# The last norm's output on ScalarE, and the message bias as a row of the state

## The reference

```python
x = _layernorm(x + adj @ (x @ W0) + b0)            # first layer
x = _layernorm(x + fused_gcn(x[:, :25], adj))      # second, on 25 "nodes"
x = _layernorm(x + attention(x, adj))              # third: u = adj*exp(e+f+a_b), h' = u @ h / sum(u)
# fourth:
h = relu(bn(conv1(x))); x_conv = relu(bn(conv17(h)) + x)
s = x @ w_se.T + b_se                              # 3 features a node
A = exp(-|s_n - s_m|^2) * adj_mask
msg = relu(x @ w_msg.T + b_msg)                    # the message
x_nmp = A @ msg
z, r, n = gru(concat(x_conv, x_nmp), x)
x = _layernorm(x + (1 - z) * n + z * x)            # the last norm, the output
```

## Time and profile before

| | |
|---|---|
| median of 3 runs | 595.26 us (595.21 to 595.3) |
| profiled execution | 594.41 us |
| its span in the trace | 592.6 us |
| TensorE clock granted | 0.996 of full speed |
| busy share | PE 97%, DVE 83%, ACT 52%, POOL 19% |

### The profile page before, as it was taken

The page is one execution under the profiler, slowest core; times in us unless marked ns, Lnnn a source line. Parts: engine busy times, 40 slices in busy tenths (PEclk is TensorE's granted clock), DMA queues, the critical chain, the costliest instruction groups (busy, mean ns, idle before and its releaser), DMA issues.

```text
span 592.6 us, 11756 instructions
## 1 busy us (share of the span) xinstructions
PE 572.8 (97%) x3611; PEld 491.2 (83%) x3611; DVE 492.8 (83%) x1842; ACT 310.4 (52%) x641; POOL 112.8 (19%) x124
## 2 busy tenths in 40 slices
PE   6998999999999999999999999999999999999894
PEld 6896987978889797979788897979797988889584
DVE  3778968898989888888989898888889898989675
ACT  2316636546464555555554646465556556464342
POOL 3311130212112030212031211203020312112010
PEclk9999999999999999999999999999999999999998
DMA  7880041020020303030301103030303021000000
GB/s 187 288 284 2 2 145 49 2 79 32 19 89 0 107 0 107 0 107 0 104 3 42 65 0 107 0 107 0 107 0 105 2 66 42 19 2 0 19 19 18
DMA packets 33309, 34.47 MB, mean 58 GB/s; under 512 B 1668, under 2 KB 22539, under 8 KB 33154
## 3 DMA queue, kind: packets, MB, share of 16 engines
q1 hardware_dynamic: 32994, 34.01, 18.3%
q10 hardware_dynamic: 288, 0.13, 0.1%
HBM read 29.75 MB, written 4.39 MB: 58 GB/s over the span
## 4 chain that ended last, share of the span: by engine, by line
PE 81%; DVE 4%; issue 1%; ACT 0%; POOLq 0%; POOL 0%; DVEq 0%
PE bank L254 13%; PE bank L256 13%; PE bank L255 13%; PE bank L1757 9%; PE pair L254 6%; PE pair L256 6%; PE pair L255 6%; PE bank L1588 4%; PE bank L1599 2%; PE pair L1688 2%; PE bank L1693 2%; PE pair L1749 2%; PE bank L1653 1%; PE bank L1699 1%; PE bank L1683 1%
## 5 line engine op out<-in xcount | busy, mean ns | idle before, releaser
L1134 POOL TENSOR_TENSOR rs<-ve,neg_half 128x4 f32<-128x4 f32 (+1 forms) x60 | 57.1, 952 | 294.0 <-DVE ve L1309 261.1
L254 PE MATMUL bank<-cd_hi,w_hi 128*128 128x256 f32 x272 | 77.4, 285 | 0.0
L255 PE MATMUL bank<-cd_lo,w_hi 128*128 128x256 f32 x272 | 76.6, 282 | 0.0
L256 PE MATMUL bank<-cd_hi,w_lo 128*128 128x256 f32 x272 | 76.3, 281 | 0.0
L1757 PE MATMUL bank<-P,msg 128*128 128x512 f32 x128 | 58.6, 600 | 1.0
L254 PE MATMUL pair<-aT_hi,x_hi 128*128 128x512 f32 x128 | 52.6, 411 | 0.6 <-DVE x_lo L772 0.3
L254 PEld LDWEIGHTS bank<-cd_hi,w_hi 128*128 128x128 f32 x272 | 51.3, 189 | 1.5
L255 PEld LDWEIGHTS bank<-cd_lo,w_hi 128*128 128x128 f32 x272 | 51.3, 189 | 1.3
L256 PEld LDWEIGHTS bank<-cd_hi,w_lo 128*128 128x128 f32 x272 | 51.4, 189 | 0.0
L256 PE MATMUL pair<-aT_hi,x_lo 128*128 128x512 f32 x128 | 50.3, 393 | 0.0
L255 PE MATMUL pair<-aT_lo,x_hi 128*128 128x512 f32 x128 | 50.1, 391 | 0.0
(11 more groups left out here) (361 smaller groups left out, 1521.3 us busy)
## 6 DMA issues: line engine op xcount, KB each, us to landing
adj_nat<-in_adj_dram SPq DMA_DIRECT2D x16, 1024.0 KB, 5.9
x_nat<-in_x_dram SPq DMA_DIRECT2D x16, 256.0 KB, 2.9
xt<-in_x_dram SPq DMA_DIRECT2D x3, 1280.0 KB, 11.8
out_dram<-y_out SPq DMA_DIRECT2D x15, 256.0 KB, 2.4
hw<-in_L_gnn_W_dram SPq DMA_DIRECT2D x2, 640.0 KB, 6.7
xt<-in_L_gnn_conv_w_dram SPq DMA_DIRECT2D x1, 1088.0 KB, 10.2
aT<-in_adj_dram SPq DMA_DIRECT2D x5, 96.0 KB
nat_ih<-in_L_gnn_w_ih_dram SPq DMA_DIRECT2D x1, 384.0 KB, 6.0
```

What stands on the lines that cost most here:

```text
L254: nc.tensor.matmul(o, lh, rh, start=start, stop=False)
L255: nc.tensor.matmul(o, lh, rl, start=False, stop=False)
L256: return nc.tensor.matmul(o, ll, rh, start=False, stop=stop)
L1134: g.tensor_tensor(rs[i][:, 0:n], ve[i][:, 0:n], neg_half[:, 0:n], ALU.pow).then_inc(po_rs[i], 1)
```

## The change

There are two parts. In the turns in which graph b-1 and graph b are both there (1 to 15), ACT writes the last norm's output as an Identity with a scale `rs` and a bias `shift` for each node; DVE computes `less`, the negative means, directly behind the variances, and POOL multiplies `less` by `rs` into `shift`. PE and SP wait for ACT's output where they waited for DVE's. And the biases of message and s move into the weights: feature 0 of the state is replaced by the constant 1 (`x3M`, made by ACT from `x3T` with a scale and a bias for each partition), row 0 of the weights is replaced by the bias, and row 0's weight is subtracted from the other 127 rows, since the features sum to zero. So the two bias matmuls go, and the waits ahead of them move behind `out0`. In the first block two small loads come in among the early ones (`b_msg` as one more row of `vrows`, `b_se` as a column), eight small loads at the end of SP's list go, and so do one ACT and two DVE instructions that made `msg_bias`; three DVE instructions come in that prepare the weights, and on POOL two memsets go, one comes in, and two small instructions make `keep`.

```diff
+                sp.dma_start(vrows[BMSG:NROWS, :], a["L3_gnn_b_msg"].unsqueeze(0)).then_inc(q_row, 16)
+                sp.dma_start(vrows[HB:BMSG, :], a["L1_gnn_b1"]...).then_inc(q_row, 16)
...
+                sp.dma_start(nat_ws[0:3, 0:1], a["L3_gnn_b_se"].unsqueeze(1)).then_inc(q_ww, 16)
...
-                sp.wait_ge(q_zero, 2)
-                for row in (0, 32):
-                    for c in range(2):
-                        sp.dma_start(msg_bias_f[row:row + 1, c, 0:D], a["L3_gnn_b_msg"].unsqueeze(0)).then_inc(q_mbf, 16)
-                        sp.dma_start(msg_bias_f[row:row + 1, c, D:D + 3], a["L3_gnn_b_se"].unsqueeze(0)).then_inc(q_mbf, 16)
...
+                v.tensor_scalar(nat_wm[:, 1:D], nat_ww[:, 1, 1:D], nat_ww[:, 1, 0:1], None, ALU.subtract)
+                v.tensor_copy(nat_wm[:, 0:1], cols[:, BMSG:BMSG + 1])
+                v.tensor_scalar(nat_ws[0:3, 1:D], nat_se[0:3, 1:D], nat_se[0:3, 0:1], None, ALU.subtract).then_inc(q_sc1, 1)
...
 (POOL, in a turn)
                 if prev and cur:
                     inverse_root(V, 0, 3)
+                    pool.wait_ge(po_rs[3], V(0))
+                    pool.wait_ge(dv_less, V(0))
+                    g.tensor_tensor(shift[:, :], less[:, :], rs[3][:, :], ALU.mult).then_inc(po_shift, 1)
...
 (ACT, in a turn: behind the tanh of the gates, ahead of the copy into agg_sb)
+                if cur:
+                    wait(act, ac_x3T, V(1))
+                    s.activation(x3M[:, :], x3T[par][:, :], ACT.Identity, bias=keep[:, 1:2], scale=keep[:, 0:1]).then_inc(ac_x3M, 1)
...
                     exponential(0)
                     exponential(1)
+                if prev and cur:
+                    wait(act, po_shift, V(0))
+                    wait(act, o_out, outs)
+                    wait(act, dv_less, V(0))
+                    for c in range(NC):
+                        last = s.activation(y_out[:, c, :], X_BANK[:, ch(c)], ACT.Identity, bias=shift[:, c:c + 1],
+                                            scale=rs[3][:, c:c + 1])
+                    last.then_inc(ac_out, 1)
...
 (DVE, in a turn)
                     statistics(3, V, 0, lambda c: X_BANK[:, ch(c)], EPS / 4)
+                    v.tensor_scalar(less[:, :], mv[3][:, :, 0], -1.0, None, ALU.mult).then_inc(dv_less, 1)
...
-                def output():
-                    hold(dve, o_out, outs)
-                    normalise(3, V, 0, lambda c: y_out[:, c, :], lambda c: X_BANK[:, ch(c)], dv_out)
-
-                if prev and not nxt:
-                    output()
...
-                if prev and nxt:
-                    output()
...
 (PE, in a turn)
-                    for o in ms_banks(nxt):
-                        t_.matmul(o[:, 0:2 * DM], ones_r[:, :], msg_bias[:, :, :].rearrange("p c d -> p (c d)"),
-                                  start=True, stop=False)
...
-                        last = t_.matmul(o[...], x3T[par][:, ch(c)], wmsT, start=False, stop=(c % 2 == 1))
+                        last = t_.matmul(o[...], x3M[:, ch(c)], wmsT, start=True, stop=True)
...
-                        wait(pe, dv_out, V(0))
+                        wait(pe, ac_out, V(0))
```

More of the change, by code:

```diff
@@ L90, in network_kernel @@
         w_lo = sb("w_lo", [128, NW, 128], f32r)
-        msg_bias = sb("msg_bias", [128, 2, DM], f32r)
-        ones_r = sb("ones_r", [128, 128], f32r)
+        keep = sb("keep", [128, 2])
+        x3M = sb("x3M", [128, N])
         cols = sb("cols", [128, NROWS])
@@ L180, in network_kernel @@
         x3T = [sb(f"x3T{i}", [128, N]) for i in range(2)]
+        less, shift = sb("less", [128, NC]), sb("shift", [128, NC])
         x3T_hi = sb("x3T_hi", [128, N], f32r)
@@ L395, in _ @@
                                 pattern=[[NODES, PJ], [0, NODES]], channel_multiplier=-1).then_inc(q_bd, 1)
-                for tile_, value in ((neg_half[:, :], -0.5), (ones[:, :], 1.0), (f(ones_r[:, :]), 1.0), (c1[:, :, :], 0.0),
+                for tile_, value in ((neg_half[:, :], -0.5), (ones[:, :], 1.0), (c1[:, :, :], 0.0),
                                      (plainT[:, 0, D:DX], 0.0), (f(G[:, :, :, :]), 0.0), (U0[:, NG:, :], 0.0)):
-                    g.memset(tile_, value)
-                g.memset(msg_bias_f[:, :, :], 0.0).then_inc(q_zero, 1)
+                    last = g.memset(tile_, value)
+                last.then_inc(q_zero, 1)
                 pool.wait_ge(q_ident, 1)
@@ L1069, in network_kernel @@
         nc.all_engine_barrier()
[L1071 removed]
+        pe_x3T, ac_x3Thi, ac_x3T, ac_x3M, dv_x3Tlo = [sem(n) for n in ("pe_x3T", "ac_x3Thi", "ac_x3T", "ac_x3M", "dv_x3Tlo")]
         pe_c1, pe_hn, pe_ms = sem("pe_c1"), sem("pe_hn"), sem("pe_ms")
@@ L1674, in turn @@
                           True, True).then_inc(pe_hn, 1)
-                    if nxt:
-                        wait(pe, dv_w, V(0))
-                    else:
-                        wait(pe, dv_y3, V(1))
-                    wait(pe, dv_P[2], V(0))
-                    wait(pe, ac_x3T, V(1))
-                    wait(pe, dv_x3Tlo, V(1))
-                    for o in ms_banks(nxt):
-                        t_.matmul(o[:, 0:2 * DM], ones_r[:, :], msg_bias[:, :, :].rearrange("p c d -> p (c d)"),
-                                  start=True, stop=False)
                 if nxt:
@@ L1690, in turn @@
                 if cur:
+                    if nxt:
+                        wait(pe, dv_w, V(0))
+                    else:
+                        wait(pe, dv_y3, V(1))
+                    wait(pe, dv_P[2], V(0))
+                    wait(pe, ac_x3M, V(1))
+                    wait(pe, dv_x3Tlo, V(1))
                     for c in range(NC):
                         o = ms_banks(nxt)[c // 2]
-                        last = t_.matmul(o[:, DM * (c % 2):DM * (c % 2) + D + 3], x3T[par][:, ch(c)], wmsT,
-                                         start=False, stop=(c % 2 == 1))
+                        last = t_.matmul(o[:, DM * (c % 2):DM * (c % 2) + D + 3], x3M[:, ch(c)], wmsT,
+                                         start=True, stop=True)
                     last.then_inc(pe_ms, 1)
```

43 lines of the change are left out of this document (20 added, 23 removed).

## The result

The changed kernel takes 586.4 us (median, 585.93 to 587.87) where the kernel before took 595.24 beside it: a ratio of 0.9854, with a 95% interval of 0.984 to 0.9868. In two later comparisons on other occasions the same kernel gave 0.9879 (0.9853 to 0.9905) and 0.986 (0.9838 to 0.9883), so the gain is 7 to 9 us.

A forecast was written before the change was run, and what follows sets the result against it. PE, busy 97%, was taken to bound the kernel, with DVE nearly as critical; 5.2 us from turns 1 to 13, 0.24 from turn 0, 0.76 from turn 14, less 0.4, made 5.8: 595.26 to 589.5 us, range 587.4 to 592.8.

The forecast's parts named there:

- turn 14: Turn 14: PE's first gate gets `xc_lo` earlier, 0.36 us on top of a turn's 0.40, a gain of 0.76.
- turns 15 and 16: Last two turns: turn 15 held by the unmoved first convolution, gain 0 (at most 0.24); turn 16 not changed.
- first block: First block: two more DMA issues delay `xt`, for which PE already waits; cost 0.4 us, between 0 and 0.65.
- the sum of a turn: Turns 1 to 13: output wait plus bias matmuls less `less`, 0.40 us a turn, 13 times 5.2.
- PE's wait at the message product: Between `out2` and the message product: PE's wait for DVE's output goes, gaining 0.24 us a turn.
- `less` at 0.08: On DVE ahead of `x_hi` and `x_lo`: the new instruction delays `agg2` by 0.08 us, between 0.05 and 0.17.
- The two bias matmuls: Ahead of `out0`: removing them saves PE 0.24 us a turn, kept because DVE's `x1` moves forward too.
- The gap at `agg2`: Between last tap and first `agg2`: grows from 0.16 and 0.25 us to about 0.25 and 0.33.
- The first (592.8): Rival: `x3M` overruns ACT's hole, `x1` does not move, `agg2` takes the bias gain back; 592.8 us, chance 0.11.
- The second: Rival: ACT stands waiting for `shift`, delaying the copy for `out2`; kernel slower, about 603 us, chance 0.05.
- The third (587.3): Rival: DVE does not hold `agg2` and `less` is hidden; 0.56 us a turn, 587.3 us, chance 0.08.
- The fourth: Rival: PE's wait at the message product has another cause and stays; 592.8 us, chance 0.04.

The follow-up runs named there:

- e3: The changed kernel run again unedited; 587.58 us, ratio 0.9879 to the kernel before.
- e1: The changed kernel with the two bias matmuls put back, so only the output's move to ACT remains; 591.08 us, ratio 0.9933 to the kernel before.
- e5: The changed kernel with one more wait: PE's message product also waits for DVE's last weighted adjacency; 601.53 us, ratio 1.0097 to the kernel before.
- e6: The changed kernel with two more small DVE instructions behind `less`, writing an unused tile; 588.85 us, ratio 0.9884 to the kernel before.
- e11: The changed kernel with `less` computed on POOL behind the root, not on DVE; 586.59 us, ratio 0.9854 to the kernel before.
- e2: The changed kernel with the output put back on DVE, so only the bias part remains; 590.82 us, ratio 0.9941 to the kernel before.
- e4: The changed kernel with its two new small loads moved behind the large loads of `xt`; 586.78 us, ratio 0.9873 to the kernel before.
- e12: The changed kernel unedited once more, in the last set of comparisons; 587.01 us, ratio 0.986 to the kernel before.
- e7: The changed kernel with POOL's root done a second time ahead of the multiply that makes `shift`; 592.55 us, ratio 0.9949 to the kernel before.
- e9: The changed kernel with only the first quarter of DVE's scaled state ahead of the last norm's aggregation; 584.03 us, ratio 0.9808 to the kernel before.
- e8: The changed kernel with all of DVE's `x_hi` and `x_lo` ahead of the last norm's aggregation; 591.58 us, ratio 0.9933 to the kernel before.
- e10: The changed kernel with the first quarter of the scaled state moved ahead and the two small loads moved late; 584.01 us, ratio 0.9812 to the kernel before.

## Why the prediction was right, and where it was not

The direction and the mechanisms were right; the sum was too small by 2.1 us of span. It is made against e3 (592.6 - 584.7 = 7.9 us), where the prediction had 5.8:

| gain in us | predicted | measured |
|---|---|---|
| turns 1 to 13, each | 0.40 | 0.52 |
| all 13 | 5.2 | 6.7 |
| turn 14 | 0.76 | 0.67 |
| turn 0 | 0.24 | 0.16 |
| turns 15 and 16 | 0 | 0.33 |
| first block | -0.4 | 0.05 |
| span | 5.8 | 7.9 |

**The step that failed is the sum of a turn, "0.24 + 0.24 - 0.08 = 0.40".** Its first term, PE's wait at the message product, was read rightly as a stall of 0.24 and mis-sized as a gain: e1 and e5 show that a stall there costs its length and 0.074 more, in the first matmul behind it, so taking it away brought 0.307. The trace of before had this already: in turn 0, without the wait, the product takes 3.43 us (95.85 to 99.29), in turn 9 it takes 3.51, and I compared only the distances ahead of it. Its last term, `less` at 0.08, is 0.03 to 0.05 (e1, e6, e11). Together 0.11 a turn, 1.4 to 1.5 us of the 2.1; the first block and the last turns make the rest. The range failed with it: I had bounded the turn's gain at 0.48 and the whole at 7.4 us, and did not doubt that a stall is worth its length. The wider range that I gave ended 7.9 us below 595.26, where the spans put the gain; that the median fell 1.0 us outside it is no more than three comparisons of medians differ by (6.9 to 8.8).

*The two bias matmuls* gave 0.235 (e2), as said, and for the reason given: `x1` moved forward by the same amount, and PE kept the gain at `agg2`. *The gap at `agg2`* should have grown by 0.08 and did not: `less` took only 0.04, and `x1` starts 0.28 earlier, not 0.24. *`x3M`* cost nothing, at 0.84 us against 0.78; the copy behind it ended as the relu began. *`y_out`* took 1.51 us and was hidden. *POOL's multiply* took 0.54 us (between my 0.2 and 1.1), and nothing waited.

*Turn 14.* Three gains should have met there. The first gate no longer waits, but the gates' next step does:

```profile
546.36 0.39 PE L259 MATMUL bank<-xc_hi,w_lo 128*128 128x512 f32 x1
546.77 0.50 PE L257 MATMUL bank<-nmp_hi,w_hi 128*128 128x512 f32 x1
547.10 0.40 PE L258 MATMUL bank<-nmp_lo,w_hi 128*128 128x512 f32 x1
```

The matmul at 546.77 comes 0.41 behind its forerunner, not 0.23, and the next 0.33 behind it: 0.28 of the gain went into another wait. It is for `nmp_lo`, which DVE makes from the message product's result behind ACT's `nmp_hi`; PE's wait for it stands ahead of all three matmuls of that step:

```profile
546.02 0.69 DVE L1337 TENSOR_TENSOR nmp_lo<-bank,nmp_hi 128x512 fp32r<-128x512 f32 x1 [0.24 <-ACT nmp_hi L1278]
546.77 0.19 PEld L257 LDWEIGHTS bank<-nmp_hi,w_hi 128*128 128x128 f32 x1 [0.46 <-DVE nmp_lo L1337]
```

I had priced the wait that went and not the next one.

*The first block.* No run shows the term of -0.4. The wait for `xt` varies from 0 to 1.06 us in ten profiles with the same loads (e4), so neither my 0.4 nor nothing can be told from it. The block as a whole came out 0.05 shorter in e3 and 0.2 longer in the first profile, since its start moves by more than that from one execution to the next.

*Turns 15 and 16* gave 0.33 where I had 0, at most 0.24. e1 has 0.18 of it and e2 0.05; no run was made to find where.

*From span to median.* The prediction took the sum off the median of 595.26, 0.85 above the profiled time of before. Three comparisons of medians gave 8.8, 6.9 and 8.4 us for the same two kernels, so the 1.0 us by which the forecast's miss of 3.1 exceeds the 2.1 of span needs no cause of its own. The granted clock of each execution sorts them: the 14 executions of before at 0.995 or 0.996 that were timed with the experiments took 594.3 us in the mean, the six of the changed kernel (result, e3 and e12) 586.4, 7.9 less, as the spans have it; the 20 and 7 at a lower clock took 595.9 and 587.5. For the three executions behind 595.26 the clock is not on record.

*The rivals.* The first (592.8) is refuted by e2. The second did not happen, and e7 shows that it would have, had `shift` come 0.74 us later. The third (587.3) came nearest in time, by luck: `less` was half hidden, but DVE does hold `agg2` (e6, e9), and the 0.085 that PE loses there did not come back. The fourth is refuted by e1.

## What to carry to other kernels

A short stall of the engine that bounds the kernel is worth its length and its restart: compare the row of the matmuls behind it with the same row where no stall stands ahead, and look at when the weights' load (PEld) starts, since there the loss shows even where the matmuls stand no further apart. Before an order is changed to feed such an engine earlier, ask how much of the work its first instruction needs: a quarter moved ahead gained 0.18 us a turn (e9), where all of it lost 0.28 (e8). And a wait that is removed from a turn of a pipeline leaves the next one in line; price that too.

## What the runs showed of the hardware

- PE behind a wait: the first matmul takes 0.07 us more to the next one at the message product (0.504 and 0.430 us, behind stalls of 0.23 and 0.80 alike), 0.08 at `agg2` (0.306 and 0.229, with a stall of 0.15 or of none), 0.105 at `out2` in e7 (0.215 and 0.110). In each pair the weights' load starts later against its matmul, by 0.08, 0.09 and 0.11 us. The clock was at its full 2.4 GHz in all of these rows.
- An instruction of 128x4 behind another on DVE costs 0.04 to 0.08 us, though its row says 0.16; POOL's multiply of that size takes 0.54 us in the changed kernel, e1, e4 and e5, 0.28 in e11, 0.26 in e9 and e10 and 0.20 in e6, e7 and e8. I did not find why.
- DVE can slip in the first turn behind the loop with nothing to wait for. In e11:

```profile
495.43 0.18 DVE L1318 BATCH_NORM_AGGREGATE mv<-st 128x2 f32<-128x6 f32 x1
495.86 0.31 DVE L1318 BATCH_NORM_AGGREGATE mv<-st 128x2 f32<-128x6 f32 x3 [0.25 <-issue]
```

The slip is there once in e1, e4, e6 and e11, whose turn 13 is 0.35 to 0.41 us longer than their turn 12, and not in before, e2, e3 and e12; it was not looked into further.
- For 3.4 us of turn 15 TensorE's clock is at half in six of the 14 profiles (the changed kernel in two of three, e5, e7, e10, e11), which makes 1.2 us; the wait of 1.95 us ahead of it is in all of them. What decides it stays open.
